# Batch 3's norm sums spread between evictions on ScalarE, its v behind the fourth tile's first product, and VectorE's layer norm of batch 3 one tile on

## What is computed

```python
def _L0_xattn_ref(teacher_logits, teacher_features, Wq, bq, Wk, bk):
    query = jnp.einsum('bnc,dc->bnd', teacher_features, Wq) + bq
    key = jnp.einsum('bnc,dc->bnd', teacher_features, Wk) + bk
    attention = jax.nn.softmax(jnp.einsum('bnd,bmd->bnm', query, key), axis=-1)
    return jnp.einsum('bln,bmn->blm', teacher_logits, attention)

def _L0_ffn_ref(inputs, ln_w, ln_b, W1, b1, W2, b2):
    x = bf16_round(inputs)
    h = mx_layernorm(x, ln_w, ln_b)     # (x - mean) * rsqrt(var + eps) * w + b
    h = mx_linear(h, W1, b1)            # mx_quant: blocks of 32 share an exponent
    h = mx_gelu(h)
    h = mx_linear(h, W2, b2)
    return bf16_round(x + h)

x = x + _L0_xattn_ref(_layernorm(x), ctx, ...)      # x1
x = x + _L0_ffn_ref(_layernorm(x), ...)             # v = layernorm(x1), input of the FFN
```

## Time and profile before

| what | value |
|---|---|
| median of 3 executions | 285.61 us (285.0 to 285.69) |
| profiled execution, its own time | 283.25 us |
| its span, first to last instruction | 281.4 us |
| PE busy | 228.7 us (81%) |
| DVE busy | 249.2 us (89%) |
| ACT busy | 169.4 us (60%) |
| POOL busy | 69.0 us (25%) |
| mean granted TensorE clock | 0.927 |

### The profile page before, as it was taken

One profiled execution on the slowest core, in us unless ns is written; L12 is line 12 of the kernel. 1 busy time (PEld: TensorE's weight loads), 2 busy tenths in 40 slices (PEclk: granted clock), 3 DMA queues, 4 the chain that ended last, 5 costly groups with the idle time before them and its releaser, 6 DMA issues.

```text
span 281.4 us, 3244 instructions
## 1 busy us (share of the span) xinstructions
PE 228.7 (81%) x937; PEld 99.4 (35%) x946; DVE 249.2 (89%) x377; ACT 169.4 (60%) x287; POOL 69.0 (25%) x96
## 2 busy tenths in 40 slices
PE   7748739996998059651699969799999989999993
PEld 7314313443433024210244433344444434444431
DVE  2388999999988899999979999599999999877992
ACT  2337216628995447845987599966566554665610
POOL 1058100022004500053060050413333233333400
PEclk9985886999999759975899999999999999999999
DMA  4963999999997952939623045635355555555683
GB/s 157 378 250 89 227 279 201 297 238 194 263 257 190 221 91 38 222 59 194 124 52 62 0 93 70 119 62 123 88 122 129 130 130 131 130 130 114 139 178 130
DMA packets 103077, 42.92 MB, mean 152 GB/s; under 512 B 93844, under 2 KB 96152, under 8 KB 102552
## 3 DMA queue, kind: packets, MB, share of 16 engines
q1 hardware_dynamic: 100224, 35.93, 58.6%
q10 hardware_dynamic: 2360, 6.83, 7.7%
q0 software_dynamic: 480, 0.02, 0.1%
HBM read 15.48 MB, written 4.19 MB: 70 GB/s over the span
## 4 chain that ended last, share of the span: by engine, by line
DVE 45%; PE 25%; ACT 11%; DMA 8%; issue 5%; POOL 4%; SPq 2%; ACTq 0%; DVEq 0%; POOLq 0%
DVE amax L764 12%; PE ps L722 9%; PE ps L712 8%; PE ps L661 4%; DVE w_int L807 4%; DMA xhl<-pf 3%; DVE hq L966 3%; DVE stats L918 3%; DMA wst<-in_L_ffn_W 3%; DVE vw L961 3%; DVE pf L871 3%; DVE phl L942 2%; DVE wquant L861 2%; POOL rs L350 2%; DVE xhl L954 2%
## 5 line engine op out<-in xcount | busy, mean ns | idle before, releaser
L661 PE MATMUL ps<-pT,xT 128*128 128x512 f16 x192 | 49.7, 414 | 14.1 <-DMA pT<-phl 11.0
L722 PE MATMUL ps<-w2T,xhl 128*128 128x512 bf16 x247 | 56.5, 379 | 2.9 <-DMA xhl<-pf 2.4
L712 PE MATMUL ps<-w1T,cxT 128*128 128x512 bf16 x256 | 58.0, 380 | 0.0
L558 ACT ACTIVATE wst<-ps 128x1024 bf16<-128x1024 f32 x32 | 32.3, 1019 | 27.9 <-PE ps L712 27.9
L764 DVE TENSOR_REDUCE amax<-phl 128x64 f32<-128x2048 bf16 x16 | 36.5, 2280 | 6.9 <-ACT phl L562 6.9
L649 PE MATMUL ps<-qkT 128*128 128x512 f32 x32 | 19.5, 715 | 22.7 <-ACT pf L457 18.8
L661 PEld LDWEIGHTS ps<-pT,xT 128*128 128x128 f16 x192 | 19.9, 106 | 48.0 <-issue 31.8
L722 PEld LDWEIGHTS ps<-w2T,xhl 128*128 128x128 bf16 x256 | 24.6, 98 | 33.2 <-DMA xhl<-pf 4.2
L712 PEld LDWEIGHTS ps<-w1T,cxT 128*128 128x128 bf16 x256 | 23.7, 98 | 32.6 <-issue 6.2
L562 ACT ACTIVATE phl<-wst 128x2048 bf16<-128x2048 bf16 x16 | 30.6, 1910 | 1.3
L423 POOL TENSOR_TENSOR wst<-wst,vs 128x512 bf16<-128x512 bf16 x12 | 14.8, 1233 | 55.5 <-DVE wquant L866 55.5
(11 more groups left out here) (79 smaller groups left out, 357.4 us busy)
## 6 DMA issues: line engine op xcount, KB each, us to landing
wst<-in_L_ffn_W ACTq DMA_DIRECT2D x6, 1024.0 KB, 6.1
xs<-in_x SPq DMA_DIRECT2D x4, 1024.0 KB, 8.4
out_x<-wst SPq DMA_DIRECT2D x16, 256.0 KB, 2.8
cx<-in_ctx SPq DMA_DIRECT2D x4, 512.0 KB, 5.8
wst<-in_L_ffn_W SPq DMA_DIRECT2D x2, 1024.0 KB, 10.3
xhl<-pf SPq DMA_TRANSPOSE x17, 4.3
xT<-xhl SPq DMA_TRANSPOSE x16, 4.6
pT<-phl SPq DMA_TRANSPOSE x16, 3.3
```

Source lines behind the costliest of these rows:

```text
L558: act.activation(ys[:, k, 1024 * g:1024 * g + 1024], ps_y[:, 2 * g:2 * g + 2, :], ACT.Copy)\
L661: pe.matmul(ps_pv[:, t % 2, :], xT[:, t, NT * a + n, :], pT[:, :, NT * c + n, :], start=(s == 0), stop=False)
L712: last = pe.matmul(ps_y[:, c, :], h1T[:, k, t, :], w1T[:, 4 * c:4 * c + 4, t, :], start=False, stop=(t == KT - 1))
L722: last = pe.matmul(ps_z[:, k, :], h2T[:, k, t, :], w2T[:, t, :], start=False, stop=(t == FT - 1))
```

## The change

On ACT, the four squares of batch 3 are split in two pairs around tile 2's `y_out`. Tile 3's `y_out` comes ahead of the four `v_out`. `z_out` of tile 0 and `y_out` of tile 4 follow. The four `v_sums` no longer stand together: the first is behind `y_out` of tile 4, the second behind `z_out` of tile 1, the last two behind `y_out` of tile 5 and ahead of `z_out` of tile 2. On POOL, `factors_v` of batch 3 stands behind both residual steps of tile 0 and ahead of those of tile 1. On DVE, tile 12's part of the layer norm is in the slot of tile 5, those of 13 and 14 in the slot of tile 6, that of 15 together with the batch's amax, power, scale and inverse in the slot of tile 7; over, clip and mult stay in the slot of tile 8. No operation is added or removed.

```diff
--- before.py
+++ after.py
@@ -414,7 +414,6 @@
             factors_v(B - 2)
             mean_x1(B - 1)
             factors_x1(B - 1)
-            factors_v(B - 1)
 
             def add_residual(i):
                 m, k = i // 2, i % 2
@@ -429,6 +428,8 @@
                 pool.tensor_tensor(os_[:, k, :], xs[:, i, :], ws[:, k, :], ALU.add).then_inc(o_rdy, 1)
 
             for i in range(T - ON_DVE):
+                if i == 1:
+                    factors_v(B - 1)
                 add_residual(i)
                 add_x(i)
 
@@ -584,22 +585,31 @@
                 y_out(0, k)
             x_plus(B - 1, 2)
             x_plus(B - 1, 3)
-            for t in range(LT):
-                x1_square(B - 1, t)
+            x1_square(B - 1, 0)
+            x1_square(B - 1, 1)
             y_out(1, 0)
-            for t in range(LT):
-                v_out(B - 1, t)
+            x1_square(B - 1, 2)
+            x1_square(B - 1, 3)
 
             def step(m, k):
                 if not isinstance(m, int) or 2 * m + k + 3 < T:
                     y_out(*tile(m, k, 3))
                 z_out(m, k)
 
-            step(0, 0)
+            y_out(1, 1)
             for t in range(LT):
-                v_sums(B - 1, t)
-            step(0, 1)
-            with act.Fori(1, T // 2 - 2) as m:
+                v_out(B - 1, t)
+            z_out(0, 0)
+            y_out(2, 0)
+            v_sums(B - 1, 0)
+            z_out(0, 1)
+            v_sums(B - 1, 1)
+            y_out(2, 1)
+            v_sums(B - 1, 2)
+            v_sums(B - 1, 3)
+            z_out(1, 0)
+            step(1, 1)
+            with act.Fori(2, T // 2 - 2) as m:
                 for k in range(2):
                     step(m, k)
             for m in range(T // 2 - 2, T // 2):
@@ -1115,7 +1125,7 @@
             slot(0, 1, parts[LT + 1])
             slot(1, 0, [])
             parts = tail_parts(B - 1)
-            parts = [[], parts[0], parts[1] + parts[2]] + parts[3:]
+            parts = [[], [], parts[0], parts[1] + parts[2], parts[3] + parts[LT], parts[LT + 1]]
             for i in range(3, 3 + len(parts)):
                 slot(i // 2, i % 2, parts[i - 3])
             slot(LT, 1, [])
```

## The result

The changed kernel took 285.63 us and the kernel before 283.55 us, each the median of 22 executions. The ratio is 1.0077, with a 95% interval of 1.0052 to 1.0102: **0.8% slower**, some 2.2 us (the medians differ by 2.1). One of the changed kernel's 22 executions took 352.0 us at a granted clock of 0.65, and the ratio compares only executions near the fastest of each kernel. The sign and the way there were as forecast.

What follows compares the result with a forecast made beforehand. DVE's chain was taken to bound up to 231.38 us, then PE's. Terms +0.15, -2.9 (old wait), +1.9 (gelu), +2.15 (factor), +2.1 (port) gave 3.4 us on 285.61: 289.0 us, range 285.9 to 290.4.

Steps and rivals of the forecast that it cites:

- The port: Slot 5: POOL's two residual operations of tile 1 hold up times_w, plus_b or over on DVE, 2.1 us.
- the level: Base of the forecast time: median of the runs 2.36 us above the profiled execution, 285.61 us.
- the shift: Slot 8 on DVE, and with it the end, comes 3.4 us later.
- Slot 4's wait goes: DVE's 2.84 us wait for tile 4's gelu, ahead of its work on tile 4, vanishes with 1.2 us to spare.
- Tile 5's gelu is late next: Bound by PE behind tile 1's second product, it ends at 187.7 us; DVE waits 1.9 us for it.
- no change: Rival: tile 1's transpose lands in 4.3 us, half a port wait or none; 285.6 to 286.4 us; chance 0.17.
- The factor's wait: In slot 5 DVE's times_w waits 2.15 us for batch 3's factor from POOL, ready at 193.4.
- DVE's sum: Adding up DVE's slots 5 to 7, ending at 199.05, 207.65 and 217.65 us; slot 8 keeps 8.7 us.
- TensorE's waits: PE idles 4.9 us in all, spread over the second products of tiles 6, 7 and 8.
- The time: Median of the changed kernel's runs: 285.61 + 3.4 = 289.0 us.
- the rival with one residual: Only one of POOL's two residuals, or neither, costs DVE; shift 1.3 to 2.4 us, 286.9 to 288.0; chance 0.30.

Runs made afterwards that it cites:

- r_pool2: Changed kernel with batch 3's second factor on POOL behind tile 1's residuals too, instead of only tile 0's; ratio 1.003 to the kernel before.
- r_pool_undone: Changed kernel with POOL's part undone, batch 3's factor ahead of all residuals; ratio 1.021 to the kernel before.
- r_mid: Changed kernel with tile 14's sums ahead of tile 5's evictions and POOL's factor behind tile 1's residuals; ratio 1.001 to the kernel before.
- r_before_d: The kernel before, unchanged, fourth trace; tile 8's second product 80.01 us behind slot 0's amax, no ratio given.
- r_dve_alone: Kernel before with only VectorE's part of the change, batch 3's layer norm one tile on; ratio 1.005 to the kernel before.
- r_sums_early_b: Changed kernel with all four pairs of sums earlier on ScalarE, first repeat of that version; ratio 0.999 to the kernel before.
- r_y3_first: Kernel before with only tile 3's evictions and gelu put ahead of the four v; tile 8's second product 80.52 us behind slot 0's amax.
- r_after_again: Changed kernel, unchanged, measured again; ratio 1.013 to the kernel before.
- r_dve_undone: Changed kernel with VectorE's part undone, tile 12's norm in slot 4 again; ratio 1.019 to the kernel before.

## Why the prediction was right or wrong

The mechanism was right: one wait gone, two new ones and the port in slot 5, a shift that stays to the end. What failed is the size of two terms. The larger is the level, the step "the median of the runs stands 2.36 above the profiled one, so 285.61 + 3.4": over 22 executions that median stands 0.30 above it, at 283.55. The smaller is the shift, 3.4 us where the trace shows 2.43, mostly because tile 1's transpose was taken to land in 5.0 us and took 4.3. On the level of 283.55 the same shift and range would have been 286.9, from 283.8 to 288.3, which holds 285.63.

Positions are again behind slot 0's amax; those of the prediction are its times less 152.25.

- **Slot 4's wait goes.** Right: 27.65 both by forecast and trace.
- **Tile 5's gelu is late next, bound by TensorE behind tile 1's second product.** Right in kind; forecast 35.45, measured 34.58. The step that was mis-sized is "It was issued at 171.75; nothing ahead of it moves. So it ends at 180.47". The issue did have its old time (19.5), but the landing was 0.7 us shorter. I had taken the landing in the earlier trace rows for a constant, though the transpose in the earlier trace rows took 4.30 us. I had put the shorter landing among the rivals, in the case "no change", where it alone was too little to reach it. Why it was shorter stays open (the landing, above).
- **The factor's wait.** Forecast 2.15 us, measured 2.13. It was 2.13 or 2.14 in all five traces with this order on ScalarE and VectorE, whatever stood around it on POOL.
- **The port.** Forecast 2.1 us, measured 1.83 (r_pool2) and 1.86 for the second pair (r_pool_undone). Of the two instructions that were to wait, one was another: `times_w` waited 0.9 us and then the scale, a small instruction with one input, 0.95. `plus_b` found the port free. By the lock that the Trainium skill describes (SBUF — State Buffer, "SBUF: two separate sides") a two-input instruction waits for a GpSimd operation that reads SBUF and began first; the trace agrees, with `times_w` at 1.64 us. The same section of the Trainium skill also lets a VectorE instruction take part if it runs in a mode that uses both ports. Whether the scale does is not shown here; the trace shows only that it took 1.17 us beside L428.
- **DVE's sum.** Slots 6, 7 and 8 were forecast at 8.6, 10.0 and 8.7 and were 8.59, 10.07 and 8.71.
- **The shift.** Forecast 3.4 us (3.37 by the sum), measured 2.43 in the trace. Of the 0.94 us between them 0.83 is slot 5's start, which follows tile 5's gelu (35.45 and 34.62), 0.17 the port and other parts of slot 5, and -0.07 slot 7.
- **TensorE's waits.** Forecast 4.9 us over tiles 6, 7 and 8, measured 4.32. Tile 5's matmuls were not 0.5 but 1.31 us early (177.62 - 149.67 against 181.51 - 152.25), so the same working gives 2.43 + 0.96 + 1.31 = 4.70; TensorE's own work from there to tile 8 took the remaining 0.38 us more than before.
- **The time.** 289.0 was 3.4 above what was measured. 1.3 of it is the shift, 3.4 against the medians' 2.1. The other 2.1 us is the level: I had put the shift on 285.61, the median of three executions, and with 22 the same kernel has 283.55. The executions of the kernel before lie between 280.6 and 287.8 us. On 285.61 the ratio of 1.0077 would be 287.8, inside the range. The profiled execution of before, 283.25, was the better base. The range had been made only from what the change might do, with nothing for the level. So the bands of time can't tell the cases apart: 285.63 lies within that of the rival "no change" (285.6 to 286.4), and the shift within that of the rival with one residual (1.3 to 2.4 us), but what either describes did not happen. The kernel is slower beyond the interval, and both residuals met VectorE's work.

## What to carry over

Price a reordering by the slot that will ask, and by the instruction that will answer, and look at which work stands between them: here the sums stood behind the very gelu that started the slot, so the wait was 2.13 us where 2.15 was forecast, though that gelu came 0.9 us sooner than forecast. Before a step is put behind another on POOL, look at what of VectorE's it will then run beside: the same two residuals cost 1.85 us beside the norm, and beside an amax at most 0.15 us, at the power behind it (0.35 us instead of 0.20). When the spans of two traces differ by less than the executions do, count from an event ahead of the change; and when the level is a median of three, widen the range by the spread of the runs.

## What the runs showed of the hardware

- Small instructions of VectorE are held by POOL as well: the scale over 128 columns, 0.22 us in most places, took 1.17 us while POOL's f32 addition of 512 columns ran. The reverse holds for POOL's operations over 4 columns: the mean (L376) took 0.88 us beside VectorE's mult and 0.23 in the earlier trace rows, the subtraction (L384) 1.18 us beside it in r_mid and 0.20 in the changed kernel.
- TensorE's granted clock in the tail's beginning varies between executions of one program. The first such difference is seen in the windows view over tile 0's first product (columns: stretch, length, busy time of TensorE and its loads, VectorE, ScalarE, POOL, then granted clock and DMA share), of the third trace of the kernel before and of the fourth:

```profile
138.33:142.13 3.80, 3.80 (x22) 1.74 (x19) 3.66 (x4) 2.63 (x8) 2.50 (x3) 1.00 0.11 23
```

```profile
142.21:146.01 3.80, 3.80 (x14) 1.43 (x11) 3.66 (x4) 1.75 (x7) 2.50 (x3) 0.55 0.11 22
```

  At 0.55, near the lower of its two levels (1.2 GHz against 2.4), 14 instructions are in the stretch instead of 22. ScalarE's first gelu ends 2.6 us ahead of the anchor instead of 4.2, slot 4's wait is 3.71 us instead of 2.84 (some 4.3 was expected), and the place 80.01 instead of 79.13. TensorE had been idle for some 9 us ahead of the attention products just before, in all of these traces. In r_before_d VectorE doesn't see the difference until slot 4. Three of the 18 traces have it at this place: r_before_d, r_dve_alone and r_sums_early_b.
- The same happened later in the tail, at other products in other traces: 5.31 us instead of 3.63 in r_dve_alone (tile 3's first product), r_y3_first (tile 5's) and r_pool_undone (tile 7's), 4.80 us in r_after_again and 5.57 us in r_dve_undone (second products of tiles 7 and 4, behind waits of 2.73 and 5.03 us). Whether the place moves depends on who is the bound: in r_dve_undone and r_pool_undone it stayed 8.39 us behind slot 9, as in the kernel before, in r_after_again and r_y3_first it came 8.79 and 8.94 us behind it.
- Slot 0's amax came between 149.67 and 154.41 us in the traces of programs that are the same up to there. That is twice the effect of the change. Among the four traces of the kernel before it spreads by 3.9 us and the whole execution by 4.8 us (281.55 to 286.33).
